# DLRM interaction tower: eleven feature multiplies spread differently among sixteen Gram units

## The reference

```python
e = jnp.stack([tbl_0[ids[:, 0]], ..., tbl_26[ids[:, 26]]], axis=1)      # 2048 x 27 x 128
interactions = jnp.einsum('bfd,bgd->bfg', e, e)
z = jnp.concatenate([e.reshape(B, -1), interactions[:, _TRIU_I, _TRIU_J]], axis=1)
h = jnp.concatenate([z, dense_ctx], axis=1)                             # 3823 columns
h = jnp.maximum(h @ W_top1 + b_top1, 0.0)                               # 512
h = jnp.maximum(h @ W_top2 + b_top2, 0.0)                               # 256
y = h @ W_top3                                                          # 1
```

## Time and profile before

| | us |
|---|---|
| median of 3 runs | 593.57 |
| lowest, highest | 593.42, 594.05 |
| the profiled execution | 594.05 |
| its span in the trace | 591.9 |
| busy: PE / PEld / DVE / ACT / POOL | 535.1 / 481.0 / 350.8 / 233.5 / 414.2 |

### The profile page before, as it was taken

How to read it: one execution, slowest core, us unless ns; L and a number is a source line. 1 busy time by engine, 2 the same in 40 slices (tenths; PEclk the granted TensorE clock), 3 DMA queues, 4 the chain that set the end, 5 groups by cost and what they waited for, 6 DMA issues and landing times.

```text
span 591.9 us, 7903 instructions
## 1 busy us (share of the span) xinstructions
PE 535.1 (90%) x2576; PEld 481.0 (81%) x2576; DVE 350.8 (59%) x1165; ACT 233.5 (39%) x717; POOL 414.2 (70%) x438
## 2 busy tenths in 40 slices
PE   0757999999999999999999999999999999997796
PEld 0547888898889988898998889888998889886584
DVE  2654838375674938475574838476483837566353
ACT  2554244351624344261524334261524435162341
POOL 5777777777777777777777777777777777777100
PEclk9988999999999999999999999999999999999699
DMA  7682221122211112222211122221211212121000
GB/s 232 208 271 75 54 54 51 53 54 54 54 53 52 52 51 55 53 54 53 55 50 52 52 53 54 54 55 54 53 50 52 53 53 54 54 54 49 19 0 1
DMA packets 19436, 37.80 MB, mean 64 GB/s; under 512 B 7637, under 2 KB 8661, under 8 KB 19397
## 3 DMA queue, kind: packets, MB, share of 16 engines
q0 software_dynamic: 13824, 28.34, 18.3%
q1 hardware_dynamic: 5284, 8.72, 4.4%
q10 hardware_dynamic: 288, 0.26, 0.2%
HBM read 37.28 MB, written 0.01 MB: 63 GB/s over the span
## 4 chain that ended last, share of the span: by engine, by line
PE 68%; POOL 16%; issue 6%; DVE 5%; DMA 2%; ACT 2%; POOLq 0%; ACTq 0%; DVEq 0%
POOL emb L196 16%; PE ps_acc L222 15%; PE ps_acc L223 13%; PE ps_acc L224 13%; PE ps_gram L247 9%; PE ps_acc L259 7%; PE ps_t L209 5%; PE ps_late L303 4%; DVE g_buf L485 2%; DMA emb<-in_tbl,idx 1%; DVE g_buf L491 1%; PE ps_late L296 1%; DMA idx<-in_ids 1%; PE ps_late L255 1%; ACT cols_t L396 1%
## 5 line engine op out<-in xcount | busy, mean ns | idle before, releaser
L196 POOL DMA_INDIRECT emb<-in_tbl,idx x432 | 413.5, 957 | 136.1 <-issue 128.6
L222 PE MATMUL ps_acc<-w_hi,emb_x 128*128 128x512 f32 x432 | 202.8, 470 | 1.2 <-DVE emb_x L475 1.2
L485 DVE COPY g_buf<-ps_gram 32x112 f32<-32x112 f32 x512 | 138.5, 271 | 70.3 <-PE ps_gram L247 60.9
L223 PE MATMUL ps_acc<-w_lo,emb_x 128*128 128x512 f32 x432 | 175.5, 406 | 0.0
L224 PE MATMUL ps_acc<-w_hi,emb_x 128*128 128x512 f32 x432 | 174.8, 405 | 0.0
L475 DVE TENSOR_TENSOR emb_x<-ps_t,emb_x 128x512 fp32r<-128x512 f32 (+1 forms) x112 | 74.5, 666 | 154.3 <-ACT emb_x L388 154.3
L427 ACT ACTIVATE g_buf<-ps_gram 32x112 f32<-32x112 f32 x512 | 130.3, 255 | 81.4 <-PE ps_gram L247 76.2
L222 PEld LDWEIGHTS ps_acc<-w_hi,emb_x 128*128 128x128 f32 x432 | 130.9, 303 | 9.0 <-DVE emb_x L475 4.7
L388 ACT ACTIVATE emb_x<-ps_t 128x512 fp32r<-128x512 f32 (+1 forms) x112 | 63.8, 583 | 183.1 <-PE ps_t L209 182.7
L223 PEld LDWEIGHTS ps_acc<-w_lo,emb_x 128*128 128x128 f32 x432 | 134.0, 310 | 2.4
L224 PEld LDWEIGHTS ps_acc<-w_hi,emb_x 128*128 128x128 f32 x432 | 131.8, 305 | 1.1
(11 more groups left out here) (26 smaller groups left out, 119.9 us busy)
## 6 DMA issues: line engine op xcount, KB each, us to landing
g_buf<-in_W_top SPq DMA_DIRECT2D x27, 256.0 KB, 4.0
emb<-in_tbl,idx POOLq DMA_INDIRECT x432, 2.5
w_cols<-in_W_top SPq DMA_DIRECT2D x1, 512.0 KB
w<-in_W_top SPq DMA_DIRECT2D x1, 512.0 KB
w_cols<-in_W_top SPq DMA_DIRECT2D x1, 222.0 KB
idx<-in_ids SPq DMA_DIRECT2D x1, 216.0 KB, 5.2
b_rows<-in_b_top ACTq DMA_DIRECT2D x1, 128.0 KB, 4.8
w_rows<-in_W_top ACTq DMA_DIRECT2D x1, 128.0 KB, 5.9
```

The lines of the kernel that those rows point to most:

```text
L196: pool.indirect_dma_start(out=emb[:, f * D:(f + 1) * D], out_offset=None, in_=tables[f], in_offset=bass.IndirectOffsetOnAxis(ap=idx[:, t, ...
L222: pe.matmul(acc, emb_part(0, f), w_hi[:, f, :], start=(f == 0), stop=False)
L223: pe.matmul(acc, emb_part(0, f), w_lo[:, f, :], start=False, stop=False)
L485: last = dve.tensor_copy(target, source)
```

## The change

The table holds eleven features and not nine. It puts one ahead of most units where two stood ahead of every third one, and the loop that multiplied the two left-over features behind `layer_2` is gone. PE does the same instructions in the other order. Nothing else changes, and tile 15 keeps its order.

```diff
-            BEFORE_UNIT = [2, 0, 0, 2, 0, 0, 2, 0, 0, 2, 0, 0, 0, 0, 1, 0]
-            assert len(BEFORE_UNIT) == UNITS and sum(BEFORE_UNIT) <= NF - 4 * GF
+            BEFORE_UNIT = [2, 1, 1, 0, 1, 1, 0, 1, 1, 0, 1, 1, 0, 1, 0, 0]
+            assert len(BEFORE_UNIT) == UNITS and sum(BEFORE_UNIT) == NF - 4 * GF
...
                 if t > 0:
                     layer_2(t - 1)
-                while f < NF:
-                    multiply(t, f)
-                    f += 1
```

## The result

| | before | changed |
|---|---|---|
| median, us | 593.81 | 600.45 |
| lowest, highest, us | 593.42, 595.72 | 599.70, 602.52 |
| runs | 4 | 4 |
| ratio (95% interval) | | 1.0115 (1.0094 to 1.0136) |
| profiled execution: time, span, us | 594.05, 591.9 | 602.09, 600.0 |

The changed kernel is 1.15% slower, 6.6 us. I had forecast 18.2 us more and a time of 602 to 621. The sign is right and the size is not: the predicted loss is 2.8 times the measured one. All fifteen executions of the changed kernel on record lie between 599.3 and 602.5 us, with a median of 601.2; the table has the four that belong to the ratio. The code before these lines moved by four lines, so L475 is now L471, L485 is L481, L491 is L487 and L388 is L384.

A forecast was written before the change was run, and what follows sets the result against it. PE and DVE set the pace until tile 14, the last gather the end in tile 15. Growth 15 x 1.91 = 28.7 us less 0.4, 8.4 and 1.7 gave +18.2, 612.0 us; range 602 to 621.

The forecast's parts named there:

- POOL runs without a pause and holds the end of the kernel before: POOL, whole run: a gather every 1.26 us, 34.1 us a tile; the last gather sets the end in tile 15.
- The period is a ring over DVE, and a later low split of group 0 lengthens it by as much: Middle tiles: PE to unit 0, DVE's low splits, back to PE; split 14.76 us behind unit 0, period up 1.91 us.
- The wait of 0.77 us goes and none comes among the units: PE ahead of unit 12, each of 15 tiles: the wait for DVE's copy of unit 9, 11.5 us in all, disappears.
- Unit 13 stands 12.06 us behind unit 0: PE within a tile: units, single features and transposes priced at 11.91 us plus 0.15, which is 2.46 us later than before.
- the 0.15 that I added: PE, unit 0 to unit 13: old-order prices gave 9.45 us against 9.60 measured; the missing 0.15 was added to the new order.
- The check on the old order: PE, unit 0 to unit 13 in the kernel before: the same prices gave 9.45 us, where 9.60 was measured.
- Edges are free: PE's switches between features and units cost nothing: walk 10.0 us, period not longer, gathers hold the end at 593.6; chance 0.04.
- Tile 15 gives back 8.4 us to DVE's chain and 1.7 to the clock, and tile 14 0.4: Last tiles: waits for gathers vanish, unit 0 of tile 15 is limited by DVE, half clock goes; 8.4, 1.7 and 0.4 us.
- the case below: Lower bound: without the missing 0.15 and with single features costing half their edge, growth 1.15 us a tile, +6.8 us, 601.
- Third rival, the clock falls at each new stall: PE, features of group 0 at half clock: 2.8 us more a tile, 28 us on top, 640 us; chance 0.04.
- The end stays tied to gathers: Tile 15: POOL waits for PE's transposes, so nothing is given back and the time is 622.8 us; chance 0.03.
- The gathers hide it: Before tile 15, PE and DVE may lose 10.5 us, 0.7 a tile, with the time staying 593.6; chance 0.04.

The follow-up runs named there:

- Two versions with a period longer by 0.35 and 0.5 us: Changed table with one feature left behind `layer_2`: 593.58 us; changed kernel with DVE's transpose behind the low split of group 1: 595.49 us; kernel before 595.53 us.

## Why the prediction missed, step by step

- **POOL runs without a pause and holds the end of the kernel before:** right. Taking three gathers a tile away gave 9.3 us in medians (10.6 in spans of the profiled executions), and 10.5 were worked out. "POOL is not moved" was wrong by the 4.9 us by which the last gather came later, but unit 0 of tile 15 stood 8.4 us behind it, so this cost nothing.
- **The period is a ring over DVE, and a later low split of group 0 lengthens it by as much:** right. The split came 1.10 us later and the period grew 1.04; moving DVE's transpose took 0.55 of it away. The second wait of PE was put at 0.9 us and is 0.45.
- **The wait of 0.77 us goes and none comes among the units:** right; L247 has no wait for DVE's copies left.
- **Unit 13 stands 12.06 us behind unit 0:** wrong, 11.22. This term is the miss, 0.84 of the 0.87 us between the predicted growth of 1.91 and the measured 1.04. The units were mis-sized: ten blocks with 13 units were put at 10 x 0.30 + 3 x 0.235 = 3.71 us and took 3.04. That is 0.67 of the 0.84; the 0.15 that I added make up nearly all the rest. I had read the price of 0.30 from 328.36 to 328.66 in the earlier trace rows, where the unit stands directly behind a transpose of a group. Behind a feature a unit takes 331.93 - 331.71 = 0.22. In the changed kernel only two of the 13 take more: unit 9, behind the transposes, 0.30, and unit 0 0.32. A block of units behind a feature has no edge; a block of features has one (0.83 for one, 1.52 for two, as priced), and 0.07 us more directly behind transposes.
- **The check on the old order** gave 9.45 where 9.60 was measured, and I took that as a confirmation of the prices. It could not confirm them: the stretch has only one single unit (unit 12, in the 0.67), and its rows of three were entered at the 0.77 that one of them had measured. Their prices never tested what a unit costs alone. The 0.15 was missing in other places: two pairs of features took 1.55 and 1.61 us and not 1.52, and the row with the wait 0.06 more. I then added it to the new order, which has no pair in this stretch.
- **Edges are free** (second rival; the Trainium skill, TensorE: Matmul & The Clock Gate, Architectural detail, says that TensorE pulls weight loads ahead of matmuls in flight): wrong as a forecast, with a walk to unit 13 of 10.0 us where 11.22 was measured and 12.06 was forecast from the rows. The runs lie between. The edge of a block of features, 0.13 us, stayed as the row had it. The edge of a block of units behind a feature was zero. I had chosen between row and rule for both kinds at once.
- **Tile 15 gives back 8.4 us to DVE's chain and 1.7 to the clock, and tile 14 0.4:** right. In the profiled executions the stretch from DVE's transpose in tile 15 to unit 0 shrank from 19.7 to 10.7 us, 9.0, and the stretch behind it by 1.6.
- **Sum:** 15 x 1.91 - 10.5 = 18.2 was forecast. 15 x 1.04 = 15.6 less 9.3 gives 6.3, where 6.6 was measured. Since a fixed sum is taken off, an error of 13 us in a cost of 16 became an error of 12 in a result of 6.6.
- **Range:** the case below was a growth of 1.15 a tile, +6.8 us and 601; I had trimmed it to 602 without a row to say so. It lies close to the measured 6.6 us by luck: it halved the edges of the features, which were as priced, and did not doubt the price of a unit. With both bounded below, the growth would have been 0.4 to 1.9, and the range would have reached 594.
- **Third rival, the clock falls at each new stall:** it did so once in the profiled execution, at the longest of them in tile 1, and cost 0.8 us; in the changed kernel with 24 gathers the same wait of 2.6 us left it full. In the version with one feature behind `layer_2` it fell after a wait of 1.8 us. The 1.00 and 0.45 us waits of the later tiles left it full.
- **The end stays tied to gathers** (fourth rival): it did not. Unit 0 of tile 15 waits for DVE, and taking gathers away left the time as it was.
- **The gathers hide it** (first rival): wrong for this change, but its threshold was right in kind. Two versions with a period longer by 0.35 and 0.5 us were not slower than the kernel before.

## What to carry to other kernels

Price an instruction from a row where it has the same neighbour as in the new order. A check of such prices on the old order is worth little where the old order holds few of the pairs that the new one is made of. When two engines form a ring, follow the handover that closes it. Work left at the end of a tile may be the cover for another engine's last copies, and moving it into the tile takes the cover away even when it ends every wait there. And where another queue hides a fixed number of microseconds, carry the doubt about the large cost, in full, over to the small difference.

## What the runs showed of the hardware

A gather that POOL starts just behind DVE's `add_parts` takes longer. In the kernel before:

```profile
301.57 0.95 POOL L196 DMA_INDIRECT emb<-in_tbl,idx  x1 [0.30 <-issue]
302.82 1.67 POOL L196 DMA_INDIRECT emb<-in_tbl,idx  x1 [0.30 <-issue]
304.80 0.94 POOL L196 DMA_INDIRECT emb<-in_tbl,idx  x1 [0.30 <-issue]
...
302.78 0.90 DVE L497 TENSOR_TENSOR gram<-g_buf 128x729 f32<-128x729 f32 x1
```

```profile
ACT emb_x L388 <- remote: 115.0, 22, 19.4
DVE emb_x L475 <- issue: 98.9, 20, 18.9
...
POOL emb L196 <- remote: 35.4, 14, 5.8
...
PE ps_acc L222 <- issue: 22.3, 15, 14.3
```

The undisturbed trace has no such line for ACT, for DVE at its low splits or for POOL. Busy times of DVE, ACT and POOL differ by at most 2.1 us between the two traces, so these three were not slower; they started late, up to 19 us at a time. PE was busy for 571.6 us and not 537.9, at a mean granted clock of 0.916 and not 0.986. The cause was not found, and a comparison of a few percent cannot be made on such a chip.
